# A twelve-layer decoder kernel: another order at the seam of layers 4 and 5, and six steps of products ahead of layer 5's first way back

## The chip, the cores and the metric

The kernel is one program on one core of a Trainium2 chip. The metric is the device time of one execution in microseconds, as a median over runs. TensorE (PE) multiplies, VectorE (DVE), ScalarE (ACT) and GpSimd (POOL) do the elementwise work, and SyncE (SP) issues the transfers.

## The reference

Twelve layers act on a state of 8 blocks of 128 tokens by 256 features (fp32), each followed by a residual and a layer norm. Only two layers matter here. Layer 4 is an attention of the 256 feature columns of each block (no softmax scaling, a factor gamma). Layer 5 is a mixture of experts in two sizes:

```python
def _moe(x2d, Wg, Wu, Wd, cw):
    g = jnp.einsum('th,ehi->eti', x2d, Wg)
    u = jnp.einsum('th,ehi->eti', x2d, Wu)
    a = jax.nn.silu(g) * u * cw.T[:, :, None]
    return jnp.einsum('eti,eih->th', a, Wd)
```

It is evaluated for 32 experts of width 96 and for 16 of width 128 with shares that are sums of pairs. The shares cw come from a softmax of 32 logits of each token, of which the four largest are kept and divided by their sum.

## The kernel before

Each engine has one instruction stream, written out by hand in order; semaphores tie the streams together. Every wait is a count: `T.down.at(n)` is reached when n ways back are done. Each layer class has the methods `pe`, `dve`, `act` and `pool`, which are called layer after layer, and a layer's streams already hold the first work of the next.

**Layer 4** (`ColumnAttention`). Its loop over v (PE, ACT), i (DVE) and b (POOL) is a software pipeline. For block b the PE sums into bank 6 (`pe_values`); ACT copies the bank to `OS` (`lifted`); DVE takes four reciprocals, a product, the residual sum and the norm's statistics (`dve_end`, r = 0 to 5); POOL turns the variance into a factor (`pool_rstd`); DVE normalizes (`dve_norm`); PE transposes the block (`pe_turn_state`); ACT copies it to `XT` (`act_copy_state`). The last block is 7.

**Layer 5** (`LargeAndSmallExperts`, a kind of `Experts`) has 40 units of 128 expert columns. Its arithmetic is fp32 from rounded halves: a value is split into a rounded part and a rest, and each product is three products (`three`). So the state needs two parts per block (`X.act_block` makes the rounded one, `X.dve_block` the rest), and each unit's weights need two (`act_split`, then `pool_split`), in a ring of 4. There are 80 steps, two for each unit (512 tokens each):

- `pe_step(i)`: 12 matmuls 128x512 into two banks, gate and value; two pairs of banks alternate.
- The way there and back: ACT takes silu of the gate (`act_front`); DVE multiplies by the value (`dve_front`, into the ring `tb`) and by the token's share (`dve_weigh`, from `SH`); ACT rounds (`act_back`); DVE makes the rest (`dve_rest`).
- `pe_down(i)`: 12 matmuls 128x256, summed in banks 0 to 3 over the whole layer.

The PE's order is set by `LAG`: with LAG 3 it runs step i and then the down product of step i-3. `BEGUN = 1` says that step 0 stands in layer 4's stream. The shares come late: they need the logits of all 8 blocks, a long chain on DVE (`dve_route`), a transpose on the PE after step 1 (`pe_turn_shares`), a copy by ACT, a transfer to DRAM and transfers back that spread each row over partitions (`sp_shares`, a ring of 3). Until then DVE goes only the first part of the way for steps 0 to 3 (`behind`). Weights come in chunks of five units, in a ring of 3 chunks.

Layers 8 and 11 use the same class with LAG 2.

Of the kernel before, what the change touches and what calls it, by code (L numbers as in the profile page):

```python
# [167 lines left out]
def build(nc, A, out):  # L168
    with ExitStack() as ctx:
# [1650 lines left out]
        class ColumnAttention:  # L1820
# [57 lines left out]
            def pe(self, e):  # L1878

                T, l = self.T, self.l  # L1880
                need_room(e, l)
                for v in range(42):
                    if 0 < v < 32:
                        self.pe_scores(e, v)
                    if 1 <= v <= 32:
                        e.wait_ge(*T.copied.at(2 * v - 2))
                        for x in range(2):
                            e.wait_ge(*T.exped.at(2 * v - 1 + x))
                            t = pe_turn(e, self.E[(2 * v - 2 + x) % 4], banks[4 + x])
                        t.then_inc(T.turned.sem, 1)  # L1890
                    if v == 33:
                        self.pe_values(e, 7, range(8))
                    elif 5 <= v < 33 and v % 4 != 0:
                        self.pe_values(e, (v - 5) // 4, (range(3), range(3, 6), range(6, 8))[(v - 5) % 4])
                    if v % 4 == 1 and v >= 13:
                        pe_turn_state(e, l, v // 4 - 3)

                    if v == 33:
                        e.wait_ge(*T.exped.at(64))
                        for b in range(5):  # L1900
                            layers[5].pe_logits(e, b)
                    if v == 37:
                        layers[5].pe_logits(e, 5)
                        e.wait_ge(*T.copied.at(64))
                        layers[5].pe_step(e, 0)
                layers[5].pe_logits(e, 6)
                layers[5].pe_logits(e, 7)

            def dve_parity(self, e):
                e.wait_ge(s_c, 48)  # L1910
# [9 lines left out]
            def dve(self, e):  # L1920
                T, l = self.T, self.l
                need_room(e, l)
                for i in range(2, 83):
                    if i < 64:
                        self.dve_max(e, i)
                    b, r = divmod(i - 18, 8)
                    if i == 74:
                        for x in range(4):
                            layers[5].X.dve_block(e, x)
                    if i == 82:  # L1930
                        for x in range(4, 7):
                            layers[5].X.dve_block(e, x)
                    if 0 <= b < 8:
                        self.dve_end(e, b, r)
                    if 0 <= b - 1 < 8 and r == 0:
                        dve_norm(e, l, b - 1)

            def dve_end(self, e, b, r):

# [22 lines left out]
            def act(self, e):  # L1962
                T, l = self.T, self.l
                for v in range(42):
                    if 0 < v < 32:
                        self.act_exps(e, v)
                    if 1 <= v <= 32:
                        for x in range(2):
                            j = 2 * v - 2 + x
                            b, r = divmod(j, 8)  # L1970
                            qc, hp = divmod(r, 4)
                            e.wait_ge(*T.turned.at(v))
                            e.wait_ge(*T.valued.at(b - 1))
                            e.e.copy(self.pairs(b)[:, hp].rearrange("p h c (q n) -> p (h c) q n", q=2)[:, :, qc, :],  # L1974
                                     banks[4 + x].rearrange("p (s n) -> p s n", s=4)).then_inc(T.copied.sem, 1)
                    if v % 4 == 0 and 8 <= v <= 36:
                        b = v // 4 - 2
                        e.wait_ge(*T.valued.at(b + 1))
                        e.wait_ge(*N[l].added.at(b - 1))
                        e.e.copy(self.OS[b % 2], banks[6]).then_inc(T.lifted.sem, 1)  # L1980
                    if v % 4 == 1 and v >= 13:
                        act_copy_state(e, l, v // 4 - 3)

                    if v == 33:
                        for b in range(5):
                            layers[5].X.act_block(e, b)
                        layers[5].act_split(e, 0)
                    if v == 36:
                        layers[5].act_split(e, 1)
                        layers[5].act_split(e, 2)  # L1990
                    if v == 37:
                        layers[5].X.act_block(e, 5)
                        layers[5].X.act_block(e, 6)
                layers[5].X.act_block(e, 7)

# [28 lines left out]
            def pool(self, e):  # L2024
                T, l = self.T, self.l
                need_room(e, l)
                e.e.memset(self.VZ[1], 0.0).then_inc(T.zeroed.sem, 1)
                e.wait_ge(*T.zeroed.at(3))
                for b in range(1, 11):
                    if b < 8:  # L2030
                        self.pool_keys(e, b)
                        self.pool_values(e, b)
                    if b >= 3:
                        pool_rstd(e, l, b - 3)
                    if b == 9:
                        layers[5].pool_split(e, 0)
                        layers[5].pool_split(e, 1)
                layers[5].pool_split(e, 2)


# [12 lines left out]
        class Experts:  # L2053
# [11 lines left out]
            LAG = 2  # L2065
            BEGUN = 0
            LATE = 3

            def __init__(self, l, units, free, turn, entries, scaled_in):
                self.l, self.entries, self.scaled_in = l, entries, scaled_in  # L2070
# [1 line left out]
                self.count = count = len(units)  # L2072
                self.room = room = Room((AR0, 11312))
                rounded = Room((R1, 12288))
                self.sg, self.tb = room.ring(3, 512), room.ring(4, 512)
                self.SH, self.shT = room.ring(3, 1024), room.take(1024)
                self.c3 = room.take(8 * entries).rearrange("p (b e) -> p b e", b=8)
                c2 = 2 * count
# [95 lines left out]
            def pe_logits(self, e, b):  # L2174
                e.wait_ge(s_c, 48)
                need_xt(e, self.l, b)
                self.R.pe_block(e, b, self.router).then_inc(self.T.logits.sem, 1)

            def downs(self, i):

                late = 2 * self.count - 2
                return range(max(i - self.LAG, 0), i - 1) if i == late else (i - (2 if i > late else self.LAG),)

            def pe(self, e):
                T, c2, l = self.T, 2 * self.count, self.l
# [26 lines left out]
            def dve_front(self, e, j):  # L2212
                T = self.T
                u, n = self.steps[j]
                s, a, q = self.sg[j % 3], self.tb[j % 4], self.SH[u % 3][:, four(n)]
                if self.scaled_in:
                    if u >= self.free:
                        e.wait_ge(*self.spread[u])
# [7 lines left out]
                    e.wait_ge(*T.gated.at(j + 1))  # L2226
                    q = s
                e.wait_ge(*T.value.at(j + 1))
                e.wait_ge(*T.rest.at(j - 3))
                e.wait_ge(*T.rounded.at(j - 3))  # L2230
                if self.scaled_in and u < self.free:
                    e.e.tensor_copy(a, self.bank(j, "u")).then_inc(T.upped.sem, 1)
                else:
# [2 lines left out]
            def dve_weigh(self, e, i):  # L2236
                T = self.T
                u, n = self.steps[i]
                a = self.tb[i % 4]
                e.wait_ge(*T.upped.at(i + 1))  # L2240
                if self.scaled_in:
                    e.wait_ge(*T.silued.at(i + 1))
                    e.tt(a, a, self.sg[i % 3], ALU.mult).then_inc(T.weighted.sem, 1)
                elif u < self.free:
                    e.ts(a, a, 1.0, ALU.mult).then_inc(T.weighted.sem, 1)
                else:
                    e.wait_ge(*self.spread[u])
                    e.tt(a, a, self.SH[u % 3][:, four(n)], ALU.mult).then_inc(T.weighted.sem, 1)

            def dve_rest(self, e, i):  # L2250
                T = self.T
                e.wait_ge(*T.rounded.at(i + 1))
                e.wait_ge(*T.down.at(i - 1))
                e.tt(self.AL[i % 2], self.tb[i % 4], self.AH[i % 2], ALU.subtract).then_inc(T.rest.sem, 1)

            def dve_back(self, e, i):
                self.dve_weigh(e, i)
# [6 lines left out]

            def behind(self, j):

                return range(max(j - 1, 0), j)

            def back_first(self, j):

# [63 lines left out]
            def act_back(self, e, i):  # L2334
                T = self.T
                e.wait_ge(*T.weighted.at(i + 1))
                e.wait_ge(*T.down.at(i - 1))
                e.e.copy(self.AH[i % 2], self.tb[i % 4]).then_inc(T.rounded.sem, 1)  # L2338

            def act_run(self, e):  # L2340
                T, c2, l = self.T, 2 * self.count, self.l
# [34 lines left out]
        class LargeAndSmallExperts(Experts):  # L2376

            LAG = 3  # L2380
            BEGUN = 1

            def __init__(self, l):
                super().__init__(l, list(range(40)), 0, 1, 48, False)
# [5 lines left out]
            def rows(u):  # L2390
                return side_by_side(u, 96) if u < 24 else [(8 + u, 0, 128)]

            def behind(self, j):

                return range(0) if j < 3 else range(3) if j == 3 else range(j - 1, j)

            def dve_route(self, e, j):
                if j == 6:
# [4 lines left out]
                R.dve_logits(e, T.logits)  # L2403
                e.ts(self.clamped, R.lg, CLAMP, ALU.min).then_inc(e.sem, e.up())
                e.settle()
                R.dve_top(e, self.clamped)
                R.dve_less_max(e, T.lessmax)
                e.wait_ge(*T.lexped.at(1))
                R.dve_mask(e)
                e.red(R.s, R.ex, ALU.add).then_inc(e.sem, e.up())  # L2410
# [1429 lines left out]
```

## Time and profile before

| | us |
|---|---|
| median of 3 runs | 1991.48 |
| lowest, highest | 1989.53, 1992.45 |
| the profiled execution | 1998.52 |
| its span | 1996.4 |
| PE busy in the span | 1836.1 (92%) |
| DVE, ACT, POOL busy | 1252.2, 1002.2, 643.5 |

The profiled execution is 2.1 us longer than its span (what lies around it) and 7.0 us longer than the median of the runs. The rows' times are from the span's start. Layer 4 ends and layer 5 begins at about 820 us; layer 5 ends at about 1170 us. Helpers record most operations under their own lines: L145 is a matmul, L262 a transpose, L151 a tensor_tensor on DVE or POOL, L156 `dve_norm`'s tensor_scalar, L364 the copy to `XT`, L375 `act_block`, L1944 a reciprocal of `dve_end`, L1980 the copy of bank 6, L2313 `act_split`, L2338 the rounding of `act_back`.

### The profile page before, as it was taken

To read this page: it belongs to the slowest core of one execution; us is meant where nothing else is said; L and a number is where in the kernel's file an instruction comes from. 1 tells how busy PE (TensorE), PEld (TensorE's weight loads), DVE (VectorE), ACT (ScalarE), POOL (GpSimd) and SP (SyncE) were. 2 spreads that over 40 slices of the span, in tenths; PEclk is the share of its full clock that TensorE was granted. 3 is DMA by queue.
4 is the path that set the end of the run, shared out by engine and by line. 5 is a ranking of instruction groups with operands and counts; after the bars stand their busy time and mean duration, and the time that the engine had idled before them with its cause. 6 is when DMAs were issued, how large, how long until landed. Compare 5 with 4: busy or idle time off the path is not lost.

```text
span 1996.4 us, 30089 instructions
## 1 busy us (share of the span) xinstructions
PE 1836.1 (92%) x11144; PEld 1419.6 (71%) x11144; DVE 1252.2 (63%) x2621; ACT 1002.2 (50%) x2249; POOL 643.5 (32%) x764
## 2 busy tenths in 40 slices
PE   8998998899999798799999989887999988999997
PEld 6886776788888644588888865665888744555686
DVE  4544775577777846654444454786444566888876
ACT  3214885255555477433333323653333368888442
POOL 1204220233333401122222224542222334888522
PEclk9998997899999989899999999977999998999999
DMA  5003401201011000133333210010223101000011
GB/s 223 27 28 101 101 2 57 85 1 43 1 41 40 28 13 1 36 104 103 103 103 135 103 51 1 1 40 23 103 103 105 55 1 40 1 0 1 1 63 44
DMA packets 25623, 105.57 MB, mean 53 GB/s; under 512 B 3643, under 2 KB 9531, under 8 KB 21509
## 3 DMA queue, kind: packets, MB, share of 16 engines
q1 hardware_dynamic: 23316, 101.87, 15.0%
q0 software_dynamic: 1728, 1.58, 0.5%
q8 instruction: 89, 1.46, 0.3%
q14 instruction: 58, 0.47, 0.1%
q10 hardware_dynamic: 432, 0.20, 0.0%
HBM read 97.56 MB, written 6.07 MB: 52 GB/s over the span
## 4 chain that ended last, share of the span: by engine, by line
PE 74%; DVE 11%; ACT 9%; issue 3%; POOL 2%; DMA 1%; SPq 0%; POOLq 0%; DVEq 0%; ACTq 0%
PE ps L145 66%; PE ps L262 7%; ACT AR L148 3%; DVE AR L162 2%; DVE AR L151 1%; POOL AR L151 1%; ACT W L148 1%; DVE Y L151 1%; DVE AR L159 1%; ACT CR L148 1%; DVE X L156 1%; DVE stt L329 1%; ACT AR L1974 1%; DVE CR L162 1%; ACT CR L3307 0%
## 5 line engine op out<-in xcount | busy, mean ns | idle before, releaser
L145 PE MATMUL ps<-R 128*128 128x512 f32 (+3 forms) x4944 | 878.7, 342 | 22.3 <-ACT AR L1526 9.7
L145 PEld LDWEIGHTS ps<-R 128*128 128x128 f32 (+1 forms) x4944 | 745.0, 194 | 141.6 <-issue 18.8
L151 POOL TENSOR_TENSOR R<-W,R 128x768 fp32r<-128x768 f32 (+2 forms) x106 | 181.9, 1721 | 566.5 <-ACT R L2313 455.9
L148 ACT ACTIVATE AR<-AR 128x512 f32<-128x512 f32 (+2 forms) x584 | 276.8, 547 | 142.6 <-DVE AR L162 108.5
L151 DVE TENSOR_TENSOR AR<-ps,AR 128x512 f32<-128x512 f32 (+5 forms) x266 | 137.3, 536 | 205.0 <-PE ps L145 188.0
L2338 ACT CAST R<-AR 128x512 fp32r<-128x512 f32 x148 | 91.8, 622 | 298.4 <-PE ps L145 162.4
L145 PE MATMUL ps<-W,AR 128*128 128x256 f32 (+3 forms) x1184 | 204.0, 352 | 10.3 <-ACT AR L1544 9.0
L262 PEld LDWEIGHTS ps<-cf,AR 128*128 128x128 f32 (+5 forms) x904 | 115.3, 148 | 116.8 <-issue 55.9
L145 PEld LDWEIGHTS ps<-W,AR 128*128 128x128 f32 (+2 forms) x1184 | 153.8, 164 | 43.2 <-issue 20.8
L262 PE MATMUL ps<-cf,AR 128*128 128x128 f32 (+5 forms) x904 | 153.1, 288 | 32.6 <-ACT AR L148 10.7
L165 DVE TENSOR_TENSOR_SCAN AR<-AR,ps 128x512 f32<-128x512 f32 x128 | 154.3, 1215 | 33.5 <-PE ps L262 24.2
L151 POOL TENSOR_TENSOR AR<-AR,CR 128x512 f32<-128x512 f32 x128 | 161.5, 1275 | 36.1 <-DVE AR L165 35.5
L151 DVE TENSOR_TENSOR R<-AR,R 128x512 fp32r<-128x512 f32 x148 | 102.4, 693 | 108.7 <-ACT R L2338 108.7
L145 PE MATMUL ps<-AR 64*128 64x128 f32 (+4 forms) x1216 | 162.0, 313 | 7.7 <-DVE AR L151 7.6
L151 DVE TENSOR_TENSOR AR<-AR 128x512 f32<-128x512 f32 (+2 forms) x297 | 161.2, 544 | 4.4 <-ACT AR L148 1.3
L151 POOL TENSOR_TENSOR AR<-AR 128x512 f32<-128x512 f32 (+2 forms) x90 | 91.0, 1011 | 181.4 <-DVE AR L151 160.3
L145 PEld LDWEIGHTS ps<-AR 128*128 128x128 f32 (+2 forms) x1216 | 124.8, 186 | 32.1 <-issue 24.1
L145 PE MATMUL ps<-AR,cf 128*128 128x512 f32 x256 | 131.2, 596 | 0.1
L148 ACT ACTIVATE AR<-ps 128x512 f32<-128x512 f32 (+1 forms) x142 | 82.0, 582 | 59.3 <-PE ps L145 57.5
L155 POOL TENSOR_SCALAR rs<-mv 128x1 f32<-128x1 f32 x96 | 24.2, 252 | 237.4 <-DVE mv L331 236.5
L148 ACT ACTIVATE W<-W,AR 128x160 f32<-128x160 f32 (+2 forms) x256 | 81.6, 392 | 28.7 <-DVE AR L162 28.7
L162 DVE TENSOR_REDUCE AR<-AR 128x4 f32<-128x512 f32 (+4 forms) x149 | 92.0, 622 | 3.3 <-ACT AR L148 0.9
(204 smaller groups left out, 2154.1 us busy)
## 6 DMA issues: line engine op xcount, KB each, us to landing
W<-in_wts SPq DMA_DIRECT2D x14, 1920.0 KB, 8.1
AR<-shd SPq DMA_DIRECT2D x32, 512.0 KB, 3.6
W<-in_wts SPq DMA_DIRECT2D x4, 2048.0 KB, 8.4
AR<-shd SPq DMA_DIRECT2D x20, 384.0 KB, 3.5
W<-in_wts SPq DMA_DIRECT2D x5, 1280.0 KB, 7.4
AR<-shd SPq DMA_DIRECT2D x20, 256.0 KB, 3.9
W<-in_wts SPq DMA_DIRECT2D x2, 1536.0 KB, 7.0
AR<-shd SPq DMA_DIRECT2D x20, 128.0 KB, 3.8
```

Of the source, the lines that this page charges most:

```text
L145: return self.e.matmul(o, l, r, start=start, stop=stop, skip_group_check=True)
L148: return self.e.activation(o, i, f, bias=bias, scale=scale)
L151: return self.e.tensor_tensor(o, a, b, op)
L155: return self.e.tensor_scalar(o, a, s1, None, op0)
L156: return self.e.tensor_scalar(o, a, s1, s2, op0, op1)
L159: return self.e.scalar_tensor_tensor(out=o, in0=a, scalar=s, in1=b, op0=op0, op1=op1)
L162: return self.e.tensor_reduce(o, i, AX, op, negate=negate)
L165: return self.e.tensor_tensor_scan(o, a, b, initial, op0, op1)
L262: return e.e.transpose(o, i, ident[0:n, 0:n])
L329: e.e.bn_stats(stt[:, b, :], y).then_inc(e.sem, e.up())
L1974: e.e.copy(self.pairs(b)[:, hp].rearrange("p h c (q n) -> p (h c) q n", q=2)[:, :, qc, :], banks[4 + x].rearrange("p (s n) -> p s n", s=4) ...
L2338: e.e.copy(self.AH[i % 2], self.tb[i % 4]).then_inc(T.rounded.sem, 1)
```

## The change

In layer 4's streams:

- ACT at v = 33 first splits units 0, 1 and 2, then copies state block 5, then copies bank 6 for block 7, then rounds state blocks 0 to 5. Before, it rounded blocks 0 to 4 and split unit 0 first; the bank was copied at v = 36, and the other two splits stood behind it.
- DVE makes the rests of blocks 0 and 1 behind block 7's residual sum, and those of 2 to 6 behind block 7's norm. Before, 0 to 3 stood ahead of block 7's reciprocals and 4 to 6 ahead of its norm.
- POOL splits units 0 and 1 ahead of the factors of blocks 6 and 7, and unit 2 once block 7's norm is done.
- PE runs step 0 behind the logits of blocks 6 and 7.

In layer 5: LAG is 5 (it falls to 4, 3 and 2 at steps 20, 24 and 28, by `lag`), so that steps 1 to 5 and step 0 stand ahead of the first down product. The ring `tb` has 7 places and not 4. DVE and ACT follow two steps behind at first (`finished`) and one step behind from 24 on. In `dve_route` the difference to the maximum, which ACT's exp waits for, stands ahead of the search for the four largest. For layers 8 and 11 the new formulas give the order that they had.

```diff
@@ ColumnAttention.pe
                     if v == 37:
                         layers[5].pe_logits(e, 5)
-                        e.wait_ge(*T.copied.at(64))
-                        layers[5].pe_step(e, 0)
                 layers[5].pe_logits(e, 6)
                 layers[5].pe_logits(e, 7)
+                e.wait_ge(*T.copied.at(64))
+                layers[5].pe_step(e, 0)
@@ ColumnAttention.dve
-                    if i == 74:
-                        for x in range(4):
-                            layers[5].X.dve_block(e, x)
-                    if i == 82:
-                        for x in range(4, 7):
-                            layers[5].X.dve_block(e, x)
                     if 0 <= b < 8:
                         self.dve_end(e, b, r)
                     if 0 <= b - 1 < 8 and r == 0:
                         dve_norm(e, l, b - 1)
+                    if i == 79:
+                        for x in range(2):
+                            layers[5].X.dve_block(e, x)
+                    if i == 82:
+                        for x in range(2, 7):
+                            layers[5].X.dve_block(e, x)
@@ ColumnAttention.act
-                    if v % 4 == 0 and 8 <= v <= 36:
-                        b = v // 4 - 2
+                    if v == 33:
+                        for u in range(3):
+                            layers[5].act_split(e, u)
+                    if v % 4 == 1 and v >= 13:
+                        act_copy_state(e, l, v // 4 - 3)
+                    if v % 4 == 0 and 8 <= v <= 32 or v == 33:
+                        b = 7 if v == 33 else v // 4 - 2
                         e.wait_ge(*T.valued.at(b + 1))
                         e.wait_ge(*N[l].added.at(b - 1))
                         e.e.copy(self.OS[b % 2], banks[6]).then_inc(T.lifted.sem, 1)
-                    if v % 4 == 1 and v >= 13:
-                        act_copy_state(e, l, v // 4 - 3)
                     if v == 33:
-                        for b in range(5):
+                        for b in range(6):
                             layers[5].X.act_block(e, b)
-                        layers[5].act_split(e, 0)
-                    if v == 36:
-                        layers[5].act_split(e, 1)
-                        layers[5].act_split(e, 2)
                     if v == 37:
-                        layers[5].X.act_block(e, 5)
                         layers[5].X.act_block(e, 6)
@@ ColumnAttention.pool
-                    if b == 9:
+                    if b == 8:
                         layers[5].pool_split(e, 0)
                         layers[5].pool_split(e, 1)
+                e.wait_ge(*N[l].normed.at(8))
                 layers[5].pool_split(e, 2)
@@ Experts
+            HELD = 4
+            def lag(self, i):
+                return max(self.LAG - max(0, (i - 16) // 4), 2)
             def downs(self, i):
-                late = 2 * self.count - 2
-                return range(max(i - self.LAG, 0), i - 1) if i == late else (i - (2 if i > late else self.LAG),)
+                return range(max(i - self.lag(i - 1), 0), i - self.lag(i) + 1)
             def behind(self, j):
-                return range(max(j - 1, 0), j)
+                return range(self.finished(j - 1), self.finished(j))
+            def finished(self, j):
+                return max(j - max(self.lag(j) - 3, 0), 0)
@@ LargeAndSmallExperts
-            LAG = 3
+            LAG = 5
             BEGUN = 1
+            HELD = 7
-            def behind(self, j):
-                return range(0) if j < 3 else range(3) if j == 3 else range(j - 1, j)
+            def finished(self, j):
+                return super().finished(j) if j > 4 else max(j - 3, 0)
@@ LargeAndSmallExperts.dve_route
+                R.dve_less_max(e, T.lessmax)
                 R.dve_top(e, self.clamped)
-                R.dve_less_max(e, T.lessmax)
+                e.settle()
```

## Rows read from the trace of the kernel before

**Rows 1.** The chain that ended last, around layer 5: start, length, what.
```profile
847.10 322.16 PE ps L145 x1836
```
**Rows 2.** Windows: each engine's busy time, then PEclk, the granted clock.
```profile
819.00:826.00 7.00, 5.81 (x17) 4.85 (x18) 6.74 (x13) 2.01 (x5) 5.41 (x5) 0.51 0.00 0
...
846.40:853.20 6.80, 6.10 (x20) 5.38 (x21) 3.14 (x5) 2.57 (x4) 1.68 (x1) 0.50 0.46 121
...
900.00:1150.00 250.00, 250.00 (x1438) 220.75 (x1437) 118.90 (x180) 94.82 (x151) 56.00 (x31) 1.00 0.33 108
1400.00:1550.00 150.00, 150.00 (x863) 132.44 (x862) 71.04 (x108) 56.70 (x90) 33.54 (x18) 1.00 0.31 104
```
**Rows 3.** PE in order of time: start, length; in brackets idle before, releaser.
```profile
813.11 1.94 PE L145 MATMUL ps<-AR 128*32 128x256 f32 x32
...
820.19 0.69 PE L262 MATMUL ps<-cf,X 128*128 128x128 f32 x2 [2.62 <-DVE X L156]
...
821.38 5.10 PE L145 MATMUL ps<-R 128*128 128x512 f32 x12
...
835.76 1.57 PE L262 MATMUL ps<-cf,AR 128*48 128x128 f32 x8 [4.59 <-DVE AR L155]
836.98 6.93 PE L145 MATMUL ps<-R 128*128 128x512 f32 x24
```
**Rows 4.** ACT at the seam, in order of time.
```profile
810.63 0.60 ACT L1980 COPY AR<-ps 128x512 f32<-128x512 f32 x1
...
817.98 0.58 ACT L1980 COPY AR<-ps 128x512 f32<-128x512 f32 x1
818.46 1.57 ACT L2313 CAST R<-W 128x768 fp32r<-128x768 f32 x2
```
**Rows 5.** POOL at the seam, in order of time.
```profile
818.16 3.68 POOL L151 TENSOR_TENSOR R<-W,R 128x768 fp32r<-128x768 f32 x2 [2.20 <-ACT R L2313]
823.34 0.30 POOL L155 TENSOR_SCALAR rs<-mv 128x1 f32<-128x1 f32 x1 [1.51 <-DVE mv L331]
```
**Rows 6.** DVE from the seam to step 4, in order of time.
```profile
813.38 0.48 DVE L159 SCALAR_TENSOR_TENSOR AR<-AR,sm 128x256 f32<-128x256 f32 x1
...
824.36 1.94 DVE L156 TENSOR_SCALAR X<-Y,mv,rs 128x256 f32<-128x256 f32 x1
...
828.07 0.11 DVE L1609 MEMSET AR<- 128x64 f32 x1
...
833.42 0.42 DVE L151 TENSOR_TENSOR AR<-AR 128x256 f32<-128x256 f32 x1 [0.54 <-ACT AR L148]
...
835.48 0.23 DVE L155 TENSOR_SCALAR AR<-AR 128x128 f32<-128x128 f32 x1
...
844.89 0.69 DVE L151 TENSOR_TENSOR AR<-AR 128x512 f32<-128x512 f32 x1 [0.17 <-DMA AR<-shd]
...
854.40 0.69 DVE L151 TENSOR_TENSOR AR<-ps,AR 128x512 f32<-128x512 f32 x1 [2.96 <-PE ps L145]
```
**Rows 7.** DVE in block 7's end: three reciprocals, then three rests.
```profile
820.05 1.36 DVE L1944 RECIPROCAL AR<-AR 128x64 f32<-128x64 f32 x3
...
823.17 1.06 DVE L151 TENSOR_TENSOR R<-XT,R 128x256 fp32r<-128x256 f32 x3
```
**Rows 8.** POOL and DVE at the same time, in layers 3 and 5.
```profile
434.87 1.28 POOL L151 TENSOR_TENSOR R<-W,R 128x512 fp32r<-128x512 f32 x1 [2.17 <-ACT R L1519]
...
435.28 1.16 DVE L151 TENSOR_TENSOR AR<-AR 128x256 f32<-128x256 f32 x1
...
861.45 2.24 POOL L151 TENSOR_TENSOR R<-W,R 128x768 fp32r<-128x768 f32 x1 [8.07 <-ACT R L2313]
862.00 2.25 DVE L156 TENSOR_SCALAR CR<-CR 128x1024 f32<-128x1024 f32 x1
```
**Rows 9.** DVE in one period of layer 5's steady part.
```profile
950.54 0.69 DVE L151 TENSOR_TENSOR AR<-ps,AR 128x512 f32<-128x512 f32 x1 [1.40 <-PE ps L145]
...
952.63 0.69 DVE L151 TENSOR_TENSOR R<-AR,R 128x512 fp32r<-128x512 f32 x1 [0.80 <-ACT R L2338]
```

More of the change, by code:

```diff
@@ L2074, in __init__ @@
                 rounded = Room((R1, 12288))
-                self.sg, self.tb = room.ring(3, 512), room.ring(4, 512)
+                self.sg, self.tb = room.ring(3, 512), room.ring(self.HELD, 512)
                 self.SH, self.shT = room.ring(3, 1024), room.take(1024)
@@ L2214, in dve_front @@
                 u, n = self.steps[j]
-                s, a, q = self.sg[j % 3], self.tb[j % 4], self.SH[u % 3][:, four(n)]
+                s, a, q = self.sg[j % 3], self.tb[j % self.HELD], self.SH[u % 3][:, four(n)]
                 if self.scaled_in:
@@ L2228, in dve_front @@
                 e.wait_ge(*T.value.at(j + 1))
-                e.wait_ge(*T.rest.at(j - 3))
-                e.wait_ge(*T.rounded.at(j - 3))
+                e.wait_ge(*T.rest.at(j - self.HELD + 1))
+                e.wait_ge(*T.rounded.at(j - self.HELD + 1))
                 if self.scaled_in and u < self.free:
@@ L2238, in dve_weigh @@
                 u, n = self.steps[i]
-                a = self.tb[i % 4]
+                a = self.tb[i % self.HELD]
                 e.wait_ge(*T.upped.at(i + 1))
@@ L2253, in dve_rest @@
                 e.wait_ge(*T.down.at(i - 1))
-                e.tt(self.AL[i % 2], self.tb[i % 4], self.AH[i % 2], ALU.subtract).then_inc(T.rest.sem, 1)
+                e.tt(self.AL[i % 2], self.tb[i % self.HELD], self.AH[i % 2], ALU.subtract).then_inc(T.rest.sem, 1)
             def dve_back(self, e, i):
@@ L2337, in act_back @@
                 e.wait_ge(*T.down.at(i - 1))
-                e.e.copy(self.AH[i % 2], self.tb[i % 4]).then_inc(T.rounded.sem, 1)
+                e.e.copy(self.AH[i % 2], self.tb[i % self.HELD]).then_inc(T.rounded.sem, 1)
             def act_run(self, e):
```

## The prediction

> **What bounds the kernel now.** I read the chain of waits first, cut to the seam of layers 4 and 5. From 847.10 on it is nothing but PE, for 322 us [rows 1], and in 250 us of that stretch PE is busy for 250 us [rows 2]. So inside layer 5 only PE's work counts, and the work is not changed: 80 steps and 80 down products. What can be won is the time before 847.10 that is not such work, and PE's clock.
>
> Then the engines' timelines around 820 us. PE waits three times: 2.62 us for the norm of block 6, until 820.19; 4.59 us for the shares, until 835.76; and from the end of step 3 (836.98 + 6.93 = 843.91) to 847.10, 3.2 us, for the first way back [rows 1, 3]. And three times its granted clock falls behind such a pause: it is at half rate (1.2 GHz) over 819 to 826 and over 846.4 to 853.2 [rows 2]; in between step 2 too starts slowly, since 24 matmuls take 6.93 us [rows 3] where 12 at half rate take 5.10 [rows 3], so 24 at full rate 5.1. I take 2.6 us as the price of a step at 2.4 GHz, and 4.17 us for a step with its down product (24 matmuls of 1438 in 250 us) [rows 2]; a down product is then 1.6.
>
> The reader is to see two chains. One makes the shares: bank 6 copied 817.98, block 7 normed 824.36 to 826.30, DVE's route from 828.07 to 835.7 [rows 4, 6]. The other carries them back: from 835.7 to the first weigh at 844.89, that is 9.2 us, in which PE has steps 2 and 3 alone to do.
>
> **The change, part by part.**
>
> *Bank 6 earlier.* PE's sums end at 813.11 + 1.94 = 815.05 [rows 3]; a transpose and a state copy of 0.4 each stand ahead, so ACT copies at about 815.75 instead of 817.98: 2.2 us won. The three splits stand before it, from 811.23 (810.63 + 0.60) [rows 4]; at 0.8 each (1.57 for two) they end at 813.6, in a time when ACT waits for PE, and cost ACT nothing.
>
> *POOL's splits of units 0 and 1.* They now run from 812.05, 1.84 us each (3.68 for two) [rows 5], to 815.8. At 813.38 DVE has block 6's product, and behind it the residual sum, both with two operands in SBUF [rows 6]. Under a POOL split of 1.28 us such a DVE operation took 1.16 us, until 436.44, 0.29 behind POOL's end at 436.15 [rows 8]; the same operation takes 0.35 in a row of three [rows 7]. So the product waits for the first split (814.2) and the sum for the second (816.1); with 0.6 for the statistics they end at 816.75, and with POOL's 1.0 (1.1 from 823.26, where POOL is released, to 824.36 [rows 5, 6]) block 6 is normed from 817.8. Without the hold DVE would be there at 816.85. That gives 0.95 of the 2.2 back.
>
> *Block 7's end.* From the three reciprocals (820.05) to POOL's start (823.34) it took 3.3 us [rows 5, 7], of which 0.2 was a hold; now 3.05, from 818.05, to 821.1. Norm from 822.15, and as no split runs beside it 0.32 us, not 1.94: it ends at 822.45, where before it ended at 826.30 [rows 6]: 3.85 won. Step 0 out of the way of block 7's transpose wins nothing by itself: it ended at 826.48, with the norm.
>
> *The rests behind the norm.* Before, one rest stood between norm and route, and the way over PE and ACT took 826.30 to 828.07, 1.77 us. Now six rests stand there, 6 x 0.354 = 2.1 [rows 7], and POOL's split of unit 2, released by that norm, competes with them. In the trace such a POOL operation, issued at 861.45 while DVE was busy, got its turn between two DVE operations, and the next DVE operation took 2.25 us [rows 8]. So the second of the six is held for most of 1.84. Below, the bound is nothing; above, 1.85; the nearest row shows nearly all, and I take 1.8. The route starts at 822.4 + 2.1 + 1.8 = 826.3, against 828.07: 1.8 won.
>
> The Trainium skill (SBUF — State Buffer, section "SBUF: two separate sides") says that GpSimd and VectorE share one port pair as an exclusive lock, for VectorE operations with two SBUF inputs too. The trace agrees (1.16 us for 0.4). By a view without that lock the route would start at 823.5.
>
> *Route.* exp runs beside the search: its wait of 0.54 us goes [rows 6], less 0.1 for operations that no longer overlap: 0.45. The table load behind exp is off the path, since DVE is not back for silu before the route's end. Shares at 835.7 - 1.8 - 0.45 = 833.45.
>
> *Steps 0 and 1.* They wait for four and eight rests: from 824.9 and 826.3. At half rate for about 6 us, as before, both end at about 833, just when the shares are ready. If the half rate lasted, they would end at 824.9 + 2 x 5.1 = 835.1, 1.6 us late.
>
> *Six steps ahead.* PE goes on 1.25 us after the shares (836.98 against 835.72) [rows 3, 6] and does steps 2 to 5: 833.45 + 1.25 + 10.4 = 845.1. The shares are spread 9.15 us after (844.89) [rows 6]: 842.6. The first weigh stands behind `dve_front` of step 4, whose product ends at 842.5: 843.3. From weigh to down product 2.2 (844.89 to 847.10) [rows 1, 6]: T = 845.5. So the pause of 3.2 us shrinks to 0.4, and what filled it is two steps.
>
> *The weight ring.* With LAG 5, ACT's split of unit u waits for the down product of step 2u-7, which PE does behind step 2u-2, and what is queued behind it on ACT is silu. Then 0.8 for ACT and 1.85 for POOL, 2.7 in all, before step 2u can start, 4.17 us after that down product: 1.4 to spare. Silu is needed at the same distance, and DVE's way back may be held once by the split and still has 2.4 us to spare. Cost 0.
>
> *LAG 2 from step 28 on.* DVE begins step i-1's product at 950.54 and the rest of step i-2 ends at 952.63 + 0.69 = 953.3 [rows 9]: 2.8 us. PE needs it after a down product and a step, 4.17 us: 1.4 to spare. Layer 8 runs with LAG 2 and PE is busy 150 of 150 us there [rows 2]. Cost 0. The spreading transfers keep their distance of five steps.
>
> *The sum.* Before, step 4 and the first down product were done at 854.36 (DVE's 854.40) [rows 6]. After, steps 0 to 6 and that down product are done at 845.5 + 4.17 = 849.65. That is 4.7 us earlier and two steps (5.2 us) further: 9.9 us. Cross-check: shares 2.25 earlier, pause 2.8 shorter, and slow clock of 3.1 (854.36 - 847.10 - 4.17) and 1.3 in steps 2 and 3 no longer met, 9.5. The profiled execution would go from 1998.5 to 1988.6; its excess of 7.0 over the median lies in no part that I can name, so I carry the difference over: 1991.5 - 9.9 = 1981.6 us.
>
> **The rivals.**
>
> *No hold by POOL.* If DVE's rests go through and the splits cost block 6 nothing, the shares come 2.7 us earlier: gain 12.6, 1978.9. Against it speak the two holds in rows 8; for it, that they are other tile shapes and that who is first can fall either way.
>
> *The clock falls once more.* PE still pauses ahead of block 7's transpose (from 818 to 822.5, with little until 824.9), and perhaps for the shares. In the trace each pause of 2.6 us or more had a slow stretch at or behind its end. If steps 2 to 5, or the first down products, run in one, up to half of its 6.8 us is lost, and steps 0 and 1 may end 1.6 late: gain 5 to 8, 1983.5 to 1986.5. The Trainium skill (TensorE: Matmul & The Clock Gate, "What's actually happening") has an idle array clocked at 1.2 GHz until it has been busy again; it does not say which pause of this kernel does it.
>
> *Starved by LAG 2: slower.* Steps 28 to 79 are 52. If the way back came x us later than the 4.17 that it has, each would cost x: at 0.19 us a step the gain is gone, at 0.27 the time is 1995.7. It needs a way back of 4.44 us where 2.8 is shown; a POOL split across the weigh could add up to 1.85 in every second step. Against it: POOL's splits fall behind the rest in each period, and layer 8.
>
> *The reordering brings nothing, only the steps do.* If the front lead is eaten by the six rests and the clock, what stays is the pause filled, about 3: 1988.5; with a ring stall also, no change.
>
> **How the numbers follow.** The forecast (gain 9 to 11) has 0.45; no hold 0.17; the clock 0.24; only the steps 0.06; LAG 2 or ring eating all of it 0.04; slower 0.04. A change of 0.2% (4 us) is about what a measurement of this kernel can tell from none. The range goes from no hold with one slow stretch less in a later layer (a unit of about 1 us beside 1978.9) to the bad clock case: 1978.0 to 1986.5. Forecast alone: 1980 to 1983. Faster by over 0.2%: 0.91; same 0.05; slower 0.04.
>
> **What the profile would show.** ACT's copy of bank 6 near 815.8 (its place before: 817.98); the norm of block 7 at 0.3 us and near 822; a rest of some 2 us beside POOL's split behind it; the route's first memset near 826.3; PE from the shares on with at most 0.4 us idle, four steps, then a down product near 845.5; PEclk 1.0 from 834 on; PE at 250 of 250 us later. The prediction is wrong if a half-rate stretch falls on steps 2 to 7, if the rests are not held, or if PE shows idle time on DVE's rest in the steady part.

## The result, and the profile after

The changed kernel takes 1986.95 us (median of 20 runs, 1983.4 to 1991.9), the kernel before 1993.69 us beside it (20 runs, 1987.8 to 2004.1): a ratio of 0.9967, 95% interval 0.9954 to 0.9979, 6.7 us less. The forecast was 9.9 us less, 1981.6 us, and its time and range (1978.0 to 1986.5) started from a median of 1991.48 that three runs had given. The measured time lies 0.45 us above the range.

PE of the profile after, at the seam and at the one gap inside layer 5, in order of time:

```profile
822.90 0.69 PE L262 MATMUL ps<-cf,X 128*128 128x128 f32 x2 [3.65 <-DVE X L156]
...
825.30 7.63 PE L145 MATMUL ps<-R 128*128 128x512 f32 x24 [0.16 <-DVE R L151]
833.65 1.06 PE L262 MATMUL ps<-cf,AR 128*48 128x128 f32 x8 [0.72 <-DVE AR L155]
834.47 11.17 PE L145 MATMUL ps<-R 128*128 128x512 f32 x48
845.83 20.46 PE L145 MATMUL ps<-R 128*128 128x256 f32 x117 [0.20 <-DVE R L151]
...
915.00 1.22 PE L145 MATMUL ps<-R 128*128 128x256 f32 x8 [0.61 <-DVE R L151]
```

The pauses of 4.59 and 3.2 us [rows 3] are 0.72 and 0.20. Steps 0 and 1 still run partly at half rate (24 matmuls in 7.63 us), but in front of the shares, for which PE waits anyway, so nothing is lost; four steps follow in one piece, and the first down product starts at 845.83 (forecast 845.5).

ACT, DVE and POOL of the same stretch, each in order of time, which answer to [rows 4 to 7]:

```profile
811.23 2.32 ACT L2320 CAST R<-W 128x768 fp32r<-128x768 f32 x3
...
815.83 0.59 ACT L1986 COPY AR<-ps 128x512 f32<-128x512 f32 x1
```

```profile
813.49 0.81 DVE L159 SCALAR_TENSOR_TENSOR AR<-AR,sm 128x256 f32<-128x256 f32 x1
814.34 1.96 DVE L151 TENSOR_TENSOR Y<-AR,X 128x256 f32<-128x256 f32 x1
...
817.98 0.41 DVE L156 TENSOR_SCALAR X<-Y,mv,rs 128x256 f32<-128x256 f32 x1 [0.56 <-POOL rs L151]
...
822.43 0.41 DVE L156 TENSOR_SCALAR X<-Y,mv,rs 128x256 f32<-128x256 f32 x1 [0.46 <-POOL rs L151]
822.76 3.73 DVE L151 TENSOR_TENSOR R<-XT,R 128x256 fp32r<-128x256 f32 x6
826.46 0.11 DVE L1609 MEMSET AR<- 128x64 f32 x1
...
833.37 0.23 DVE L155 TENSOR_SCALAR AR<-AR 128x128 f32<-128x128 f32 x1
```

```profile
812.16 3.85 POOL L151 TENSOR_TENSOR R<-W,R 128x768 fp32r<-128x768 f32 x2 [3.42 <-ACT R L2320]
...
822.92 1.94 POOL L151 TENSOR_TENSOR R<-W,R 128x768 fp32r<-128x768 f32 x1 [0.53 <-DVE X L156]
```

Both holds are there: 1.96 us for block 6's residual sum of 0.42, and 3.73 for six rests that are 2.1 alone. The copy of bank 6 is at 815.83, the norm of block 7 at 822.43, the route at 826.46 and the shares at 833.6, each within 0.3 us of the forecast.

So the forecast gain was there at 846. Windows show where it went. I cut the trace at four DVE operations that every kernel has: the statistics of layer 4's block 5, of layer 5's block 2 and block 7, and of layer 7's last block; a fifth cut is the last statistics of the program. First the kernel before, then the kernel after; columns as in [rows 2], length first, PEclk third from the end:

```profile
807.70:1171.40 363.70, 349.87 (x2016) 306.29 (x2016) 183.31 (x316) 134.23 (x220) 78.84 (x50) 0.98 0.31 101
1192.70:1366.90 174.20, 142.54 (x687) 101.00 (x685) 117.59 (x255) 86.48 (x259) 81.57 (x98) 0.85 0.03 12
1366.90:1992.70 625.80, 580.72 (x2870) 426.15 (x2870) 424.96 (x701) 350.14 (x618) 274.61 (x262) 0.96 0.13 43
```

```profile
807.80:1163.20 355.40, 345.91 (x2016) 302.95 (x2016) 186.70 (x316) 134.26 (x220) 78.94 (x50) 0.99 0.31 104
1183.40:1360.20 176.80, 144.76 (x687) 102.12 (x685) 116.24 (x255) 86.70 (x259) 81.70 (x98) 0.85 0.03 12
1360.20:1985.90 625.70, 580.39 (x2870) 425.88 (x2870) 424.71 (x701) 350.36 (x618) 274.70 (x262) 0.96 0.13 43
```

The seam and layer 5 are 8.3 us shorter. Between the first two windows, in layer 5's last blocks, 1.0 more is won (20.3 us for 21.3), so 9.4 us of the 9.9 are there when layer 5 ends. Layers 6 and 7, whose code is not touched, take 2.6 us more. The rest is the same. The spans differ by 7.0 us (1996.4 and 1989.4).

### The profile page after: what moved, and what is told of

Same layout as the page of the kernel before. It is cut to its first block, busy times and chain, and to the rows that moved or that the text cites. A ratio compares the mean times of both kernels' runs of the same rounds, so it can differ in the third digit from the quotient of the medians.

```text
span 1989.4 us, 30085 instructions
## 1 busy us (share of the span) xinstructions
PE 1833.0 (92%) x11144; PEld 1415.7 (71%) x11144; DVE 1254.0 (63%) x2621; ACT 1003.1 (50%) x2249; POOL 643.8 (32%) x764
## 4 chain that ended last, share of the span: by engine, by line
PE 73%; DVE 12%; ACT 9%; issue 3%; POOL 2%; DMA 1%; SPq 0%; POOLq 0%; DVEq 0%; ACTq 0%
PE ps L145 66%; PE ps L262 7%; ACT AR L148 3%; DVE AR L162 2%; DVE AR L151 2%; DVE Y L151 1%; DVE AR L159 1%; POOL AR L151 1%; ACT W L148 1%; ACT CR L148 1%; DVE stt L329 1%; DVE X L156 1%; ACT AR L1974 1%; DVE CR L162 1%; DVE R L151 1%
## 5 line engine op out<-in xcount | busy, mean ns | idle before, releaser
L151 DVE TENSOR_TENSOR AR<-AR 128x512 f32<-128x512 f32 (+2 forms) x297 | 166.1, 560 | 3.7 <-ACT AR L148 0.8
```

What stands on the lines that cost most here:

```text
L151: return self.e.tensor_tensor(o, a, b, op)
```

## The experiments

Each kernel's profile was cut at the same operations. "To block 2" is the first window (layer 4's block 5 to layer 5's block 2), "passage" the second (layers 6 and 7), with the time in it for which PE's granted clock was at half rate. That time can be worked out from a row, to about 2 us: of 174.2 us at a mean clock of 0.85, 2 x 0.15 x 174.2 = 52 (the trace's own records give 51). The ratio is to the kernel before, run beside it on the same chip; the kernels are explained below it.

| kernel | to block 2 | passage | of it at half rate | ratio, 95% interval |
|---|---|---|---|---|
| before | 363.7 | 174.2 | 51 | 1 |
| changed (the result) | 355.4 | 176.8 | 55 | 0.9967 (0.9954 to 0.9979) |
| changed, again | 355.4 | 176.9 | 55 | 0.9955 (0.9938 to 0.9972) |
| changed, a third time | 355.4 | 176.7 | 55 | 0.9962 (0.9945 to 0.9980) |
| steps only | 359.2 | 183.2 | 68 | 1.0015 (0.9995 to 1.0034) |
| seam only | 360.6 | 175.0 | 48 | 0.9987 (0.9970 to 1.0004) |
| LAG 4 | 364.8 | 179.9 | 61 | 1.0014 (0.9997 to 1.0032) |
| 1.4 us more | 356.7 | 172.1 | 41 | 0.9938 (0.9915 to 0.9960) |
| 1.4 us more, again | 356.7 | 172.1 | 41 | 0.9946 (0.9924 to 0.9967) |
| 2.75 us more | 358.0 | 175.0 | 48 | 0.9981 (0.9963 to 1.0000) |
| odd falls of LAG | 355.9 | 187.0 | 75 | 1.0012 (0.9993 to 1.0031) |
| split behind rests | 355.0 | 174.9 | 44 | 0.9958 (0.9936 to 0.9979) |
| split behind route | 354.2 | 183.9 | 72 | 1.0012 (0.9996 to 1.0028) |
| the same, 0.7 more | 355.0 | 180.8 | 65 | 1.0000 (0.9978 to 1.0021) |
| before, 1.4 more | 365.1 | 177.5 | 58 | 1.0015 (0.9994 to 1.0037) |
| before, 2.75 more | 366.7 | 172.1 | 41 | 1.0013 (0.9981 to 1.0044) |

A row's profile is one execution, its ratio compares 5 to 20 runs with 17 to 31 of the kernel before. The two agree: "to block 2", layer 5's last blocks and the passage together differ from the kernel before by 6.8 us less (changed), 3.3 more (steps only), 9.0 less (1.4 us more, both times), and so on, and in all fifteen rows the ratio stands for a change within 3.4 us of that (correlation 0.94). The total of one profiled execution is a worse guide, since what lies outside these stretches differs between executions though no edit touches it. Up to the first cut all kernels run the same code, yet it took 795.8 us (LAG 4) to 808.4 (seam only), most of the difference in layer 1 (192.1 to 200.5 us), and two executions of one kernel took 800.2 and 803.3. The stretch behind the passage took 621.2 to 626.0 us.

**The changed kernel again.** No edit.

> The changed kernel itself, once more. Theory A: the seam and the six steps give about 9.5 us where the first way back begins, 8.2 to 9.3 of it are left at layer 5's end, and what is missing behind that (2.5 us in the profile) is PE's granted clock in layers 6 and 7, which falls in some executions and not in others. Then the third residual sum of layer 5 (block 2's statistics, 1162.94 in the profile after) stays within 0.2 us of its place, while the span moves between 1982 and 1990, and a profile with a short span lacks the half-rate stretch near 1232. Rival: the loss is an order of waits that every execution has; then every profile has the stretch and a span of 1989.

The layer 5 part came back to 0.1 us (355.4), and so did the passage (176.9 against 176.8). Theory A's first half holds: the gain at layer 5's end is there. Of its second half (the clock falls in some executions only) the profile shows nothing, and what the rival foretold came: the same half-rate time and a span of 1988.1 us. That rules out neither, for a reason that the times show. Six runs took 1984.4 to 1990.6 us, and in the 20 runs of the result 12 took 1983.4 to 1988.4 us at a mean granted clock of 0.950 to 0.953 and 8 took 1989.9 to 1991.9 at 0.949. All three profiled executions of this kernel (1991.3, 1990.1 and 1991.4 us) are among the long ones; where the short ones save their time no trace shows. The seventh run took 2500.0 us at a clock of 0.674, which nothing here explains.

**The two halves of the change.** "Steps only" has the edits in `Experts` and `LargeAndSmallExperts` but `dve_route`'s; "seam only" has those in `ColumnAttention` and `dve_route`.

> Only the six steps, the ring of 7 and the falling LAG; the seam and the route as before. Theory A: the shares stay at 835.7; down product 0 starts 12.2 us later, at 847.9 (up to 1.7 more if the clock is slow in steps 2 to 5), and no half-rate stretch follows it. Lead at layer 5's end 5 to 7 us. Rival (the seam is what counts, the steps only move PE's work): lead below 3 us.

> Only layer 4's new orders and the route's; LAG 3 as before. Theory A: the shares are 2.1 us earlier (833.6), the pause of 3.2 us before down product 0 stays and the half rate behind it too; lead at layer 5's end about 2.1 us, at most 3.5 if the clock falls a stretch less. Rival (the seam is what counts): 6 us or more.

PE of steps only, then of seam only, from the transposes of the shares on:

```profile
831.56 1.60 PE L262 MATMUL ps<-cf,AR 128*48 128x128 f32 x8 [4.59 <-DVE AR L155]
832.81 12.35 PE L145 MATMUL ps<-R 128*128 128x512 f32 x48
845.37 4.89 PE L145 MATMUL ps<-R 128*128 128x256 f32 x28 [0.20 <-DVE R L151]
```

```profile
834.18 1.06 PE L262 MATMUL ps<-cf,AR 128*48 128x128 f32 x8 [0.67 <-DVE AR L155]
834.99 5.70 PE L145 MATMUL ps<-R 128*128 128x512 f32 x24
844.94 11.23 PE L145 MATMUL ps<-R 128*128 128x256 f32 x49 [4.25 <-DVE R L151]
```

With the steps alone the pause of 4.59 us before the shares stays, four steps take 12.35 us instead of 11.17 since the clock is slow at their start, and the pause behind them goes. With the seam alone the first pause goes and the second grows to 4.25 us. To block 2 they win 4.5 and 3.1 us; together 8.3. At layer 5's block 7, which is nearer to its end, they lead by 5.7 and 3.2 us: the steps as expected (5 to 7), the seam above the 2.1 expected and within its bound of 3.5. Neither shows clearly in the times: both intervals of the ratio hold 1, and the steps' gain is given back in a passage 9 us longer.

**Five steps ahead.**

```diff
-            LAG = 5
+            LAG = 4
```

> The changed kernel with LAG 4, so five steps ahead of the first way back. Theory A: step 4 ends near 842.6, the spread shares land at 842.7, the way back takes 2.2, so PE pauses about 2.3 us and down product 0 starts near 844.9; one step (2.75) less is done and 0.9 us is won: 1.8 us slower than the changed kernel, 1.7 to 3.4 more if the pause brings the clock down. Rival (the sixth step is hidden anyway, the way back bounds): same as the changed kernel within 0.5 us.

PE, from the five steps on:

```profile
822.92 8.46 PE L145 MATMUL ps<-R 128*128 128x512 f32 x36
834.29 7.22 PE L145 MATMUL ps<-R 128*128 128x256 f32 x24 [2.92 <-DVE R L151]
844.34 5.85 PE L145 MATMUL ps<-R 128*128 128x256 f32 x25 [2.83 <-DVE R L151]
```

The pause is there (2.92 us for 2.3), a second one of 2.83 us follows the next step and down product, and half-rate stretches lie behind both. To block 2 it takes 364.8 us, 9.4 more than LAG 5 and 1.1 more than before; 3.5 to 5.2 more were expected, which had one pause in them and not two. The granted clock was 0.54 over 834 to 841 us and 0.73 over 841 to 847, behind the two pauses. So the sixth step is no surplus: with it PE does not pause here, and the clock was 1.00 over 829.5 to 860.

**More work, to shift the start of layer 6.** The gate product of step 40 (six matmuls), or the gate and the value product (twelve), is issued twice. The result of the layer is the same. It was done to the changed kernel and to the kernel before.

```diff
+                if self.l == 5 and i == 40:
+                    for what, o, free in (("g", 0, T.gated),):
+                        k = self.bank(i, what)
+                        e.wait_ge(*free.at(i - 1))
+                        three(e, k, wh[:, o:o + 128], wl[:, o:o + 128], xh[:, 0, sl], xl[:, 0, sl], True, False)
+                        three(e, k, wh[:, o + 128:o + 256], wl[:, o + 128:o + 256], xh[:, 1, sl], xl[:, 1, sl], False, True)
```

> The changed kernel with six matmuls of step 40 issued twice (its gate product; the result is the same), 1.4 us of PE work in the middle of layer 5. Theory A (what layers 6 and 7 take depends on when they begin against PE's clock): layer 5's end is 1.4 us later, and the total moves by something else, anywhere from 4 us less to 6 us more; the passage of layers 6 and 7 differs by the half-rate stretches in it. Rival (the missing 2.5 us are a fixed chain of waits): the total is 1.4 us later and the passage the same within 0.3 us.

> The same with all twelve matmuls of step 40 twice: 2.75 us more PE work. Theory A: again a passage of layers 6 and 7 of its own, not in line with the 1.4 us case. Rival: 2.75 us later, passage the same.

> The kernel before with six matmuls of step 40 issued twice, 1.4 us of PE work. Theory A: layer 5's end 1.4 us later, the passage of layers 6 and 7 another one than before, so that the total is not 1.4 us more: anything from 4 less to 8 more. Rival: 1.4 us more.

> The kernel before with all twelve matmuls of step 40 twice, 2.75 us. As the last one. Taken with it and with the two of the changed kernel (1980.6 with 1.4 us more, 1989.8 with 2.75 more) it gives the change's effect at three starts of layer 6: in the mean the changed kernel should be 6 to 9 us faster, where single pairs give 3 to 12.

With 1.4 us more work the changed kernel is faster, by more than the 4 us that were expected at most: a median of 1980.6, where the changed kernel without it had 1987.1, though on another chip. The passage, first of this kernel and then of the slowest one of the table (odd falls of LAG):

```profile
1178.30:1350.40 172.10, 138.29 (x687) 97.10 (x685) 117.35 (x255) 86.57 (x259) 81.55 (x98) 0.88 0.04 12
```

```profile
1178.60:1365.60 187.00, 154.71 (x687) 108.49 (x685) 118.46 (x255) 87.34 (x259) 81.54 (x98) 0.80 0.03 11
```

PE's instructions are the same 687, yet it is busy 138.3 us in the one and 154.7 in the other, and the granted clock is 0.88 against 0.80. Over all rows of the table each us more at half rate goes with 0.40 to 0.44 us more of passage (15 us between 41 and 75). The rival, a fixed chain of waits, would have left the passage as it was. The passage is not all of the 6 us: it is 4.7 us shorter than in the changed kernel, while the added work and layer 5's last blocks cost 2.4; the other 4.5 us are in the stretch behind the passage (621.2 for 625.7), whose code no edit touches either.

The last of these expectations can be read from the ratios: changed over before is 0.9962 without extra work (the third run), 0.9938/1.0015 = 0.992 with 1.4 us more, 0.9981/1.0013 = 0.997 with 2.75. The mean is 0.995, some 10 us, where 6 to 9 were expected; the single pairs give 6 to 15, with an uncertainty (95%) of 3.5 us for the first and 6 to 7 for the others, whose two kernels ran on different chips.

**Does it come back?**

> The changed kernel with six matmuls of step 40 issued twice, a second time. If what layers 6 and 7 take is set by when they begin, it is 4 to 8 us faster than the changed kernel again, with a passage of 172 us and 41 us of half rate in it; if it is a draw of each execution, it is the same as the changed kernel or 1.4 us slower.

> The changed kernel, beside it on the same chip: 6 to 8 us faster than before, passage 176.8 us with 54.5 at half rate, if set by the start; else anything.

It does: the passages were 172.1 and 176.7 us on another chip, the medians 1981.5 and 1986.2, 4.7 us apart on the same chip. So in the profiled executions the part that layers 6 and 7 take is no draw. The kernel with 1.4 us of work too much is the fastest of this study, 0.9938 and 0.9946 of the kernel before; it is no better program, and any later edit can undo that.

What selects the passage stays open. More work in front of it changes it, with all else the same. But the moment at which it begins is not enough to tell it. It begins 375.2 us behind layer 4's block 5 in three kernels (split behind rests, split behind route, the same with 0.7 more) and takes 174.9, 183.9 and 180.8 us. Nor is the moment against the clock enough: the clock first falls in the passage 48.8, 48.4 and 49.0 us behind its start in the three executions of the changed kernel, and 49.0 and 49.1 in "split behind route" and "split behind rests", which are 7 us longer and 2 us shorter.

**The gap of 0.6 us and layer 5's end.**

```diff
-                return max(self.LAG - max(0, (i - 16) // 4), 2)
+                return max(self.LAG - max(0, (i - 17) // 4), 2)
@@ dve_run
-                if l < 11:
+                if l == 8:
                     self.dve_sum(e, 1)
                 self.dve_front(e, c2 - 1)
+                if l == 5:
+                    self.dve_sum(e, 1)
```

> The changed kernel with the LAG falling at steps 21, 25 and 29 (odd) and layer 5's second residual sum behind the last multiplication by the value. Theory: PE's gap of 0.77 us behind step 21 goes, since ACT's silu no longer stands behind a split that waits for a down product two steps away, and the last product is 0.4 us less late: layer 5's end 1.1 us earlier against layer 4. Rival (the gap only moves to step 22, or is due to POOL's hold alone): lead inside layer 5 unchanged.

The gap stayed, with PE's down product at 909.85 idle before it for 0.62 us. To block 2 it took 0.5 us more and not 1.1 less: the residual sums of blocks 1 and 2 now stand behind the last multiplication by the value (1155.53 in its trace, the sums 1156.13 and 1157.44), and the norms behind them. Both edits failed, and the passage behind them was the longest of all. The rows of the changed kernel at that gap, all engines, say why the first did:

```profile
910.24 0.83 ACT L2320 CAST R<-W 128x768 fp32r<-128x768 f32 x1 [1.74 <-PE ps L145]
910.98 0.59 ACT L148 ACTIVATE AR<-ps 128x512 f32<-128x512 f32 x1
911.15 1.87 POOL L151 TENSOR_TENSOR R<-W,R 128x768 fp32r<-128x768 f32 x1 [6.44 <-ACT R L2320]
911.61 0.69 DVE L151 TENSOR_TENSOR AR<-ps,AR 128x512 f32<-128x512 f32 x1 [2.38 <-ACT AR L148]
912.22 1.36 DVE L151 TENSOR_TENSOR AR<-AR 128x512 f32<-128x512 f32 x1
913.61 0.62 ACT L2345 CAST R<-AR 128x512 fp32r<-128x512 f32 x1 [2.03 <-DVE AR L151]
914.26 0.69 DVE L151 TENSOR_TENSOR R<-AR,R 128x512 fp32r<-128x512 f32 x1 [0.69 <-ACT R L2345]
```

ACT's split waits for PE's down product and starts at 910.24, silu stands behind it, DVE behind silu, and the weigh of step 17 is held to 1.36 us by POOL's part of the same split. (It stands three steps behind the product at 911.61, step 20's, not two; in the kernel before it is one.) The rest of step 17 ends at 914.95 and PE goes on at 915.00. Whether the second down product of the catch-up stands behind step 20 or 21, the work in front of down product 17 is the same (the steps up to 21, the down products up to 16), and it is due at the same time.

**POOL's split of unit 2.** Behind the eight rests, and then behind the route, where the line below waits for `T.shares.at(1)` instead.

```diff
-                e.wait_ge(*N[l].normed.at(8))
+                e.wait_ge(*layers[5].T.xs.at(8))
                 layers[5].pool_split(e, 2)
```

> The changed kernel with POOL's split of unit 2 behind all eight rests. Theory (POOL held DVE's second rest): the six rests take 2.1 and not 3.7 us, the route starts and the shares come 1.55 us earlier, and down product 0 starts 1.5 us earlier against layer 4. Rival (the rests are slow by themselves): nothing moves.

> The changed kernel with POOL's split of unit 2 behind the route (the shares made), where DVE has nothing that it can hold back. Theory: of the hold of 1.6 us, which behind the rests only moved to the route's clamp (1.33 us instead of 0.29), nothing is left; down product 0 starts 1.5 us earlier against layer 4's sixth block than in the changed kernel (36.9 us after it, not 38.4), and layer 5's end too. Rival: step 4 then waits for unit 2's rest of the weights; the first down product is not earlier.

> The same with three matmuls of step 40 issued twice, 0.7 us of PE work more. Layer 5's end 0.7 us later than in that kernel; if the passage of layers 6 and 7 hangs on when it begins against PE's clock, it differs from it by more than the 0.7 us, in either direction; if not, the total is 0.7 us later.

DVE of the first kernel, the six rests and the route's clamp, then the clamp of the second:

```profile
821.15 2.13 DVE L151 TENSOR_TENSOR R<-XT,R 128x256 fp32r<-128x256 f32 x6
...
824.02 1.33 DVE L155 TENSOR_SCALAR AR<-AR 128x256 f32<-128x256 f32 x1
```

```profile
825.30 0.29 DVE L155 TENSOR_SCALAR AR<-AR 128x256 f32<-128x256 f32 x1
```

The rests take 2.13 us and not 3.73, as expected of the hold; but it moves to the clamp, 1.33 for 0.29, and of 1.5 us only 0.3 reach block 2. Behind the route the hold is gone, and 1.1 us reach block 2 (354.23 for 355.35). The passage took them back with 7 us more: less waiting up to layer 5's end, and a slower kernel. The quarter of a step more (0.7 us) gave 3.1 us of passage back.

## Why the prediction was wrong

- **Bank 6 earlier, POOL's splits of units 0 and 1, block 7's end, rests behind the norm, route:** right, each within 0.3 us. The shares came 2.3 us earlier for a forecast of 2.25 (25.95 us behind block 5's statistics, for 28.2 before).
- **Steps 0 and 1, six steps ahead:** right. Down product 0 at 845.83 for 845.5; a step costs up to 2.8 us (four took 11.17) rather than 2.6. No half-rate stretch behind it. By the prediction's own sum (854.36 - 845.83 - 4.17, and two steps) that is 9.6 to 9.9 us.
- **The weight ring, "Cost 0":** wrong. The slack of 2.4 us was that of the steady LAG 5. At step 20 two down products follow each other and a whole step less stands before the next; there the split costs 0.6 us of idle PE, waiting for DVE's rest, which was one of the prediction's signs of being wrong:

```profile
900.00:1150.00 250.00, 249.39 (x1445) 220.38 (x1444) 121.35 (x181) 94.88 (x151) 56.03 (x30) 1.00 0.34 116
```

 Of these 250 us PE is busy for 249.4. In all the lead is 8.65 us where both kernels have done the same work again, at the multiplication of step 25:

```profile
933.53 0.69 DVE L151 TENSOR_TENSOR AR<-ps,AR 128x512 f32<-128x512 f32 x1 [0.86 <-PE ps L145]
```

 Before, that operation was at 942.18. Some 0.3 to 0.6 us of the loss between 846 and 933 I could not place.
- **LAG 2 from step 28 on:** right for PE up to the layer's last steps (no idle shown until 1162); there it waits 1.9 us in three pieces, where before it waited 0.8 in one. 8.3 us are left at block 2, and 9.4 at block 7: the clock was at half rate for 3.4 us between the two and not 6.8, which no part of the prediction had.
- **The sum:** this is the step that failed. It carried layer 5's gain to the end unchanged, and gave layers 6 and 7 no term. They took 2.6 us more for the same instructions (176.8 for 174.2), with PE busy 2.2 us longer and at half rate for 55 us and not 51. At 0.40 to 0.44 us for each us at half rate that is about 1.5 of the 2.6; the rest stays open. The rival on the clock looked for the loss only in steps 2 to 7, where there was none; that the measured gain lies within its 5 to 8 us is luck. The experiments show that this term is as large as the change: 172 to 187 us for the same instructions, and the medians follow it. Why PE's clock falls more often in layers 6 and 7 of one kernel than of another I did not find out, and no run here predicts it.
- **The scale:** the time named was too low by 2.2 us more, since the kernel before is at 1993.69 in 20 runs and not at 1991.48. With both, 9.9 us became 6.7, and 1981.6 became 1986.95, 0.45 above the range. With either one right the time would have been inside the range: from 1993.69 the same gains give 1980.2 to 1988.7, and without the 2.6 us the time would have been near 1984.4. The excess of 7.0 us of the first profile needed no part to lie in: runs of this one kernel spread over 16 us, and that profile was one of the longer, the three runs were among the shorter ones.

The Trainium skill (SBUF — State Buffer, "SBUF: two separate sides") has the lock between VectorE and GpSimd held for a whole instruction; the runs agree, since moving the split moved the hold to what DVE did beside it, 1.6 us on the rests or 1.0 us on the clamp.

## What to carry to other kernels

Where a long stretch is bound by PE, count the pauses in front of it and the half-rate time behind each: one step too few ahead of the first way back (LAG 4) cost 9.4 us up to layer 5's block 2, where its first pause was 2.9. Read a gain by windows cut at the same operations on both sides, and expect that stretches behind it, where PE pauses often, change by several us either way when only the work in front of them got longer or shorter (here 5 us less for 1.4 us more work, 3 us more for the same in the kernel before); judge an edit with several such amounts, not one. Do not read the gain from the whole span of single profiles: stretches ahead of any edit differed by 12.6 us here. A ring or a hold that has slack in the steady state must be checked again where the order catches up.

## What was not expected of the hardware

The passage of layers 6 and 7 came back to 0.2 us in three profiled executions of one kernel (176.8, 176.9, 176.7) and in two of another (172.1, 172.1), on at least two chips each, while it differs by 15 us between kernels whose instructions there are the same. The time at half rate in it was 55 us in all three, and 41 in both. Layer 1, which nothing was changed in or ahead of, did not come back like that in the second kernel (193.2 and 196.5 us), though it did in the first (200.0 to 200.2). A kernel was made 4.7 us faster on the same chip by 1.4 us of useless matmuls 190 us ahead of the passage, and another some 9 us slower by an edit that takes 1.1 us of waiting out (ratios 0.9967 and 1.0012 of the kernel before, on different chips).
